# Moving the load of the next unit's fields from the end of a unit to behind its second layer, on three engines

## The chip, the cores and the metric

The kernel runs on one core of a Trainium2 chip. The metric is the device time of one execution in microseconds (us); lower is better. Five engines work side by side, each with an instruction stream of its own: TensorE (PE in the profile, its weight loads are PEld), VectorE (DVE), ScalarE (ACT), GpSimd (POOL) and SyncE (SP, here only DMAs). A "q" behind an engine's name (PEldq, ACTq) marks work of the engine's sequencer, which handles registers, branches and semaphore waits and hands instructions to the engine.

## The reference

The layer is a cross attention with sigmoid scores and a mixture of experts behind it, each gated and added to its input. Cut to the part in which the change lies:

```python
# M = 2048 tokens, H = 512, E = 16 experts, TOP_K = 4
t = norm(x) * norm_w
vals, idx = top_k(t @ gate_w.T + gate_b, 4)
gates = softmax(vals)                                  # scattered to G[M, E]
h = einsum('mh,eoh->emo', t, w1) + b1                  # first layer, 1024 outputs
a = minimum(h[..., ::2], 7); b = clip(h[..., 1::2], -7, 7)
act = a * sigmoid(1.702 * a) * (b + 1)                 # 512 hidden values
y = einsum('emi,edi->emd', act, w2) + b2               # second layer
out = x + tanh(g) * einsum('me,emd->md', G, y)
```

The kernel computes an expert only for the tokens that chose it.

## The kernel before, in words

The first 170 us hold the attention, the norms, the router, and the building of a table of token lists. Then comes the stage of the experts: a loop over units (`e.Fori(0, n)`, n is 24 here) that PE, ACT, DVE and POOL each run on their own. A unit is up to four tiles of 128 tokens of one expert. Because the lists are only known at run time, each engine reads a unit's fields (expert, slot of the second layer's weights, whether it is the expert's last unit, number of tiles, width, row) from a table `te` in SBUF into registers, with one load (`load_fields`, line 259). It keeps three sets of registers: `was` (the unit before), `now` and `nxt`. At the end of a unit `was` takes `now`, `now` takes `nxt`, and `nxt` is loaded with the fields of unit u + 2.

In a unit TensorE works in this order. The first layer has four parts, i = 0 to 3; a part is two groups (h = 0 and 1) of 12 matmuls (line 553; 32-bit numbers are split into a high and a low piece, so 4 x 3 products), whose width is 256 to 512 tokens. The code of a part exists once for each of six widths, and three compares and branches choose it (line 565). Inside part 0, and behind parts 0, 1 and 2, `turned_in(0..3)` turns a tile of tokens for the unit after this one (four transposes, line 479), if that unit has it. Behind part 0 stands `second_layer`, which is the second layer of the unit before: 12 matmuls of 512 columns for each of its tiles (line 500). All turned tiles go through one PSUM bank, `PX`: the transposes of tile j + 1 wait (line 477) until VectorE has read tile j out of it.

ScalarE in a unit: copy the biases (760), sigmoid part `sg` (720) and linear part `bw` (724) of part 0 with the copy of turned tile 0 (`high_x`, 683) between them; `second()`, that is the casts of the second layer's weights in a new expert (730) and then `gated` for each tile of the unit before (702, which waits for VectorE's bias add 1048); then `turned_in(1)` (683 again), the cast of a quarter of the next expert's first weights in an expert's last unit (`next_high`, 749), `kept(0)` (744), and the same for parts 1 to 3. VectorE follows it: bias add of the second layer's tiles (1048), low piece of a turned tile (`low_x`, 1023), the two steps of the activation (1075, 1077), low piece of the hidden values (`low_h`, 1081) and of the weights (1086). GpSimd gathers the tiles of tokens (1171) for `turned_in` and scatters the results (1228).

The order on each engine is that of the code; there is no scheduler. The lines that the change moves are 574 to 578 on TensorE, 778 to 782 on ScalarE and 1118 to 1122 on VectorE. GpSimd has its own set of registers and is not touched.

Of the kernel before, what the change touches and what calls it, by code (L numbers as in the profile page):

```python
# [19 lines left out]
E = 16  # L20
# [33 lines left out]
F_X, F_S2, F_LAST, F_NT, F_HL, F_ROW = range(6)  # L54
# [26 lines left out]
def build(nc, x, ctx, ctxT, gx, gf, nw, gw, gb, wts, bias, b1t, cst, out):  # L81
    with ExitStack() as es:
# [175 lines left out]
        def load_fields(e, regs, t, a):  # L258
            e.reg_load(regs, te[0:1, t:t + 1, a:a + len(regs)] if isinstance(t, int) else te[0:1, bass.ds(t, 1), a:a + len(regs)])
# [118 lines left out]
        def pe(e):  # L378
# [146 lines left out]
            with e.Fori(0, n) as u:  # L525
                par = e.snap(u % 2)
                x_ = e.snap(now[F_X], min_val=0, max_val=E - 1)
                wide = e.snap(now[F_HL], min_val=1, max_val=16)
                more = e.snap(nxt[F_NT], min_val=0, max_val=4)
                def turned_in(j):  # L530
                    with e.If(more > LESS[j]):
                        e.reg_add(turned, turned, 1)
                        e.reg_add(landed[j], landed[j], 16)
                        come, free = e.snap(landed[j], min_val=16, max_val=16 * NTILES), e.snap(turned, min_val=5, max_val=NTILES + 24)
                        e.wait_ge(d_g[j], come)
                        turn_x(j, free)

                ready = e.snap(e.snap(turned, min_val=4, max_val=NTILES + 24) + 1)
                for i in range(4):
                    made, read = e.snap(x_ * N1 + (i + 1)), e.snap(u * 4 + (i + 1))  # L540
                    e.wait_ge(e_lo1, made)
                    e.wait_ge(e_af, read)
                    e.wait_ge(e_bf, read)
                    e.sem_inc(e_gp, 1)

                    def part(w):
                        if i == 0:
                            e.wait_ge(e_xl, ready)
                        for h, P_, q in ((0, PA, e_l1a), (1, PB, e_l1b)):
                            t = 0  # L550
                            for k in range(4):
                                for xl, wl in PASSES:
                                    m = e.matmul(P_[i % 2][:, 0:32 * w], (W1h, W1l)[wl][:, i, 2 * k + h, :],  # L553
                                                 (xTh, xTl)[xl][:, bass.ds(par, 1), k, 0:32 * w], start=(t == 0), stop=(t == 11))
                                    t += 1
                            m.then_inc(q, 1)
                            if i == 0 and h == 0:
                                turned_in(0)

                    def pick(ws):  # L560
                        if len(ws) == 1:
                            part(ws[0])
                        else:
                            mid = len(ws) // 2
                            with e.If(wide <= ws[mid - 1]):
                                pick(ws[:mid])
                            with e.Else():
                                pick(ws[mid:])

                    pick(WIDTHS)  # L570
                    if i == 0:
                        second_layer(e.snap(u * 4 + 4))
                    if i < 3:
                        turned_in(i + 1)
                for a, q in zip(was, now):
                    e.reg_mov(a, q)
                for a, q in zip(now, nxt):
                    e.reg_mov(a, q)
                load_fields(e, nxt, e.snap(u + 2), 0)
            second_layer(e.snap(n * 4 + 4))  # L580


# [1 line left out]
        def act(e):  # L584
# [122 lines left out]
            with e.Fori(0, n) as u:  # L707
# [29 lines left out]
                def turned_in(i):  # L737
                    with e.If(more > LESS[i]):
                        e.reg_add(turned, turned, 1)
                        high_x(i, e.snap(turned, min_val=5, max_val=NTILES + 24), bass.ds(odd, 1))  # L740
# [21 lines left out]
                e.sem_inc(e_ga, 1)  # L762
                by_width(lambda w: gate(0, w, lambda: turned_in(0)))
                second()
                turned_in(1)
                next_high(0)

# [7 lines left out]
                        kept(i, w)  # L775

                by_width(pairs)
                for a, q in zip(was, now):
                    e.reg_mov(a, q)
                for a, q in zip(now, nxt):  # L780
                    e.reg_mov(a, q)
                load_fields(e, nxt, e.snap(u + 2), 0)
            e.wait_ge(e_dg, e.snap(n + 1))
            e.sem_inc(e_ga, 1)
            back = e.snap(was[F_NT], min_val=0, max_val=4)
# [6 lines left out]
        def dve(e):  # L792
# [257 lines left out]
            with e.Fori(0, n) as u:  # L1050
# [51 lines left out]
                turned_in(0)  # L1102
                by_width(lambda w: hidden(0, w))
                second()
                turned_in(1)

                def pairs(w):
# [7 lines left out]
                        low_w(i)  # L1115

                by_width(pairs)
                for a, q in zip(was, now):
                    e.reg_mov(a, q)
                for a, q in zip(now, nxt):  # L1120
                    e.reg_mov(a, q)
                load_fields(e, nxt, e.snap(u + 2), 0)
            side = e.snap(was[F_S2], min_val=0, max_val=1)
            back = e.snap(was[F_NT], min_val=0, max_val=4)
            come = e.snap(e.snap(was[F_X], min_val=0, max_val=E - 1) * 16 + 16)
# [171 lines left out]
```

## Time and profile before

| | |
|---|---|
| time, median of 3 runs | 821.39 us (820.71 to 821.41) |
| the profiled execution | 826.44 us, of which the span from the first to the last instruction is 824.5 us |
| PE busy | 766.4 us, 93% of the span |
| weight loads (PEld) | 653.8 us, 79% |
| DVE, ACT, POOL busy | 463.4, 417.9, 304.1 us |
| DMA | 117.02 MB, mean 142 GB/s |
| granted TensorE clock | mean 0.973; below full in one slice of the start and at the very end |

How to read it: PE is busy nearly throughout, with the other engines half busy beside it. The modelled end of a matmul lies behind the start of the next one, so a short stop of PE does not show as idle time of PE; it shows in the starts of the weight loads. In the unit loop one weight load begins for every matmul, so a stop is a distance between two starts beyond the usual one: 0.12 us at 256 columns, 0.13 at 288, 0.17 at 384, 0.20 at 448 and 0.23 at 512, read off between neighbouring weight loads. Units are counted from 0 in the texts; unit 0 begins at 173 us, unit 8 at 414, unit 11 at 497, unit 21 at 733, and unit 23, the last, at 779 us.

### The profile page before, as it was taken

The numbers are of one execution on the slowest core, as the hardware profiler recorded it, in microseconds if no ns is written. First come the engines' busy times: TensorE is split into PE (matmuls) and PEld (weight loads), VectorE is DVE, ScalarE is ACT, GpSimd is POOL, SyncE is SP. The second block draws the span as 40 slices with busy tenths as digits, with TensorE's granted clock in tenths as the row PEclk, the third lists the DMA queues.
The fourth block names the chain that finished last, engine by engine and source line by source line (L and its number), as shares of the span: only waits on it lengthen the run. The fifth ranks groups of instructions, "written<-read, shape, count | busy, mean of one in ns | idle before, by whom it ended". The sixth has DMA issues, their size and how long they took to land.

```text
span 824.5 us, 16539 instructions
## 1 busy us (share of the span) xinstructions
PE 766.4 (93%) x4067; PEld 653.8 (79%) x4068; DVE 463.4 (56%) x927; ACT 417.9 (51%) x691; POOL 304.1 (37%) x287
## 2 busy tenths in 40 slices
PE   8999996189999999999998999999999999999984
PEld 3666754178889889988887988898998888898873
DVE  3899885337556554556457555547346464646431
ACT  4577553036546454555556545537355554546431
POOL 0157766622332423421521443323342243325212
PEclk9999997599999999999999999999999999999997
DMA  8657743235757755655847864637545464544323
GB/s 288 222 191 231 237 122 113 43 105 154 168 128 225 155 124 140 127 149 156 205 92 212 216 131 102 156 99 175 127 90 144 99 181 115 159 115 76 38 26 39
DMA packets 107768, 117.02 MB, mean 142 GB/s; under 512 B 11808, under 2 KB 77344, under 8 KB 107744
## 3 DMA queue, kind: packets, MB, share of 16 engines
q1 hardware_dynamic: 88896, 77.32, 30.5%
q0 software_dynamic: 18848, 39.40, 24.7%
q8 instruction: 12, 0.20, 0.1%
q14 instruction: 12, 0.10, 0.0%
HBM read 88.06 MB, written 28.94 MB: 142 GB/s over the span
## 4 chain that ended last, share of the span: by engine, by line
PE 82%; issue 7%; DVE 3%; DMA 3%; ACT 2%; POOL 1%; ACTq 0%; DVEq 0%; POOLq 0%; another core or an unknown queue 0%; SPq 0%
PE ps L553 40%; PE ps L500 24%; PE ps L408 7%; PE ps L396 5%; PE ps L479 4%; DMA xg<-rows,srcI 2%; PE ps L425 1%; DVE W1l L1086 1%; PE ps L391 1%; PE ps L416 1%; POOL out L1228 1%; DVE bv L1075 0%; ACT bw L724 0%; DMA ys<-rows,src 0%; DVE ps L1048 0%
## 5 line engine op out<-in xcount | busy, mean ns | idle before, releaser
L553 PE MATMUL ps<-xTh,W1h 128*128 x768 | 257.8, 336 | 12.0 <-issue 6.5
L553 PE MATMUL ps<-xTh,W1l 128*128 x768 | 250.3, 326 | 0.0
L553 PE MATMUL ps<-xTl,W1h 128*128 x768 | 250.2, 326 | 0.0
L1228 POOL DMA_INDIRECT out<-ys,dgI x75 | 118.5, 1580 | 311.9 <-ACT ys L702 292.3
L553 PEld LDWEIGHTS ps<-xTh,W1h 128*128 128x128 f32 x768 | 144.6, 188 | 22.1 <-issue 17.6
L553 PEld LDWEIGHTS ps<-xTh,W1l 128*128 128x128 f32 x768 | 144.6, 188 | 5.1
L553 PEld LDWEIGHTS ps<-xTl,W1h 128*128 128x128 f32 x768 | 144.9, 189 | 4.5
L702 ACT ACTIVATE ys<-ps,dgI 128x512 f32<-128x512 f32 x75 | 51.8, 690 | 142.1 <-DVE ps L1048 138.1
L500 PE MATMUL ps<-W2h,hTh 128*128 x300 | 118.5, 395 | 3.4 <-DVE hTl L1081 3.2
L500 PE MATMUL ps<-W2h,hTl 128*128 x300 | 118.1, 394 | 0.0
L500 PE MATMUL ps<-W2l,hTh 128*128 x300 | 118.0, 393 | 0.0
L1023 DVE TENSOR_TENSOR xTl<-ps,xTh 128x512 f32 (+1 forms) x75 | 51.7, 691 | 93.4 <-ACT xTh L683 92.1
L1048 DVE TENSOR_TENSOR ps<-ps,b2s 128x512 f32<-128x512 f32 x75 | 52.4, 698 | 90.8 <-PE ps L500 89.9
L724 ACT ACTIVATE bw<-ps,bcur 128x384 f32<-128x384 f32 (+2 forms) x96 | 57.3, 596 | 86.0 <-PE ps L553 69.6
L1171 POOL DMA_INDIRECT xg<-rows,srcI x71 | 75.9, 1069 | 39.2 <-issue 37.9
L1075 DVE TENSOR_SCALAR bv<-bw 128x384 f32<-128x384 f32 (+2 forms) x96 | 35.9, 374 | 86.2 <-ACT bw L724 76.4
L1151 POOL DMA_INDIRECT tab<-C,dst x64 | 69.4, 1084 | 36.2 <-DVE dst L902 18.9
L1081 DVE TENSOR_TENSOR hTl<-hv,hTh 128x384 fp32r<-128x384 f32 (+2 forms) x96 | 55.2, 575 | 38.6 <-ACT hTh L744 33.9
L1086 DVE TENSOR_TENSOR W1l<-W1f,W1h 128x1024 fp32r<-128x1024 f32 x60 | 73.1, 1218 | 0.0
L720 ACT ACTIVATE sg<-ps,bcur 128x384 f32<-128x384 f32 (+2 forms) x96 | 57.3, 597 | 25.3 <-PE ps L553 12.8
L500 PEld LDWEIGHTS ps<-W2h,hTh 128*128 128x128 f32 x300 | 57.0, 190 | 15.6 <-issue 4.2
L500 PEld LDWEIGHTS ps<-W2l,hTh 128*128 128x128 f32 x300 | 57.0, 190 | 12.1
(147 smaller groups left out, 951.7 us busy)
## 6 DMA issues: line engine op xcount, KB each, us to landing
W1f<-in_wts SPq DMA_DIRECT2D x64, 512.0 KB
W2f<-in_wts SPq DMA_DIRECT2D x32, 512.0 KB
X<-in_x SPq DMA_DIRECT2D x8, 512.0 KB, 6.5
Kt<-in_ctx SPq DMA_DIRECT2D x8, 512.0 KB
Vt<-in_ctxT SPq DMA_DIRECT2D x8, 512.0 KB
rows<-tt SPq DMA_DIRECT2D x8, 512.0 KB
out<-base SPq DMA_DIRECT2D x8, 512.0 KB
b2s<-in_bias SPq DMA_DIRECT2D x16, 256.0 KB
```

Source lines behind the costliest of these rows:

```text
L408: m = e.matmul(ps[2 + j][:], Vt[b % 2][:, c, 128 * j:128 * j + 128], Sc[:, c, :], start=(c == 0), stop=(c == 3))
L500: m = e.matmul(PY[j][:], (hTh, hTl)[hl][:, c, 128 * j:128 * j + 128], (W2h, W2l)[wl][:, bass.ds(slot, 1), H * c:H * c + H], start=(t == 0) ...
L553: m = e.matmul(P_[i % 2][:, 0:32 * w], (W1h, W1l)[wl][:, i, 2 * k + h, :], (xTh, xTl)[xl][:, bass.ds(par, 1), k, 0:32 * w], start=(t == 0) ...
L702: e.activation(ys[j][:], PY[j][:], AF.Copy, scale=dgI[:, j, 1:2]).then_inc(e_ys, 1)
L720: e.activation(sg[i % 2][:, 0:w], PA[i % 2][:, 0:w], AF.Silu, scale=ALPHA, bias=bcur[:, 2, i:i + 1]).then_inc(e_af, 1)
L724: e.activation(bw[i % 2][:, 0:w], PB[i % 2][:, 0:w], AF.Identity, scale=1.0 / ALPHA, bias=bcur[:, 1, i:i + 1]).then_inc(e_bf, 1)
L1048: e.tensor_tensor(PY[j][:], PY[j][:], b2s[:, bass.ds(side, 1), :].rearrange("p o h -> p (o h)"), ALU.add).then_inc(e_yb, 1)
L1081: e.tensor_tensor(hTl[:, i, 0:w], hv[i % 2][:, 0:w], hTh[:, i, 0:w].bitcast(F32), ALU.subtract).then_inc(e_hl, 1)
L1086: e.tensor_tensor(W1l[:, i, :, :], W1f[:, i, :, :], W1h[:, i, :, :].bitcast(F32), ALU.subtract).then_inc(e_lo1, 1)
L1151: e.indirect_dma_start(tab, bass.IndirectOffsetOnAxis(dst[:, b, q:q + 1], axis=0), pay[:, 2 * b + q // K, q % K, :], None).then_inc(d_put, 16)
L1171: e.indirect_dma_start(xg[j][:], None, rows, bass.IndirectOffsetOnAxis(srcI[:, j, 0:1].bitcast(I32), axis=0)).then_inc(d_g[j], 16)
L1228: e.indirect_dma_start(out, bass.IndirectOffsetOnAxis(dgI[:, j, 0:1].bitcast(I32), axis=0), ys[j][:], None, compute_op=ALU.add).then_inc(d ...
```

## The change

Register moves and the load of `nxt` leave the end of the loop's body and stand behind the second layer (TensorE, in part 0) and behind `second()` (ScalarE, VectorE). What is read from `now` and `nxt` after that point is read from `was` and `now`.

```diff
@@ pe
                     if i == 0:
                         second_layer(e.snap(u * 4 + 4))
+                        for a, q in zip(was, now):
+                            e.reg_mov(a, q)
+                        for a, q in zip(now, nxt):
+                            e.reg_mov(a, q)
+                        load_fields(e, nxt, e.snap(u + 2), 0)
+                        x_ = e.snap(was[F_X], min_val=0, max_val=E - 1)
+                        wide = e.snap(was[F_HL], min_val=1, max_val=16)
+                        more = e.snap(now[F_NT], min_val=0, max_val=4)
                     if i < 3:
                         turned_in(i + 1)
-                for a, q in zip(was, now):
-                    e.reg_mov(a, q)
-                for a, q in zip(now, nxt):
-                    e.reg_mov(a, q)
-                load_fields(e, nxt, e.snap(u + 2), 0)
@@ act, and the same in dve
                 second()
+                for a, q in zip(was, now):
+                    e.reg_mov(a, q)
+                for a, q in zip(now, nxt):
+                    e.reg_mov(a, q)
+                load_fields(e, nxt, e.snap(u + 2), 0)
+                x_ = e.snap(was[F_X], min_val=0, max_val=E - 1)
+                nt = e.snap(was[F_NT], min_val=1, max_val=4)
+                more = e.snap(now[F_NT], min_val=0, max_val=4)
+                last = e.snap(was[F_LAST], min_val=0, max_val=1)
                 turned_in(1)
...
                 by_width(pairs)
-                for a, q in zip(was, now):
-                    e.reg_mov(a, q)
-                for a, q in zip(now, nxt):
-                    e.reg_mov(a, q)
-                load_fields(e, nxt, e.snap(u + 2), 0)
```

TensorE, around the second layer: the last matmul of its fourth tile, the branch out of it, and the first turned tile behind it (`C` and `xg` are the identity and the gathered tokens).

```order
 L500 MATMUL ps<-W2l,hTh 128x512
 L488 UNCONDITIONAL_BRANCH
+L574 ISA x2
+L576 ISA
+L259 TENSOR_LOAD te
+L578 ISA
 L531 COMPARE_AND_BRANCH
 L532 ISA
 L479 MATMUL ps<-C,xg_66 128x128 x4
```

The load now stands between the second layer and the transposes of `turned_in(1)`, with four register instructions around it.

TensorE, at the end of the loop's body, behind the last matmul of part 3:

```order
 L553 MATMUL ps<-xTh,W1l 128x512
 L567 UNCONDITIONAL_BRANCH
-L576 ISA
-L578 ISA x2
-L259 TENSOR_LOAD te
 L525 REGISTER_ALU
 L525 COMPARE_AND_BRANCH
```

What is left there is the loop's own counting and branch.

ScalarE, behind `gated` of the fourth tile (`ys`), before the change:

```order
L702 ACTIVATE ys_64<-ps,dgI 128x512
L734 UNCONDITIONAL_BRANCH
L738 COMPARE_AND_BRANCH
L739 ISA
L683 ISA
L683 COPY xTh<-ps 128x4x128
```

and after it (lines of the changed file; 702, 734, 738, 739 and 683 have become 705, 737, 741, 742 and 686):

```order
L705 ACTIVATE ys_64<-ps,dgI 128x512
L737 UNCONDITIONAL_BRANCH
L769 ISA
L259 ISA
L259 TENSOR_LOAD te
L773 ISA
L741 COMPARE_AND_BRANCH
L742 ISA
L686 ISA
L686 COPY xTh<-ps 128x4x128
```

The load stands between the last `gated` and the copy of turned tile 1 out of `PX`; on VectorE it stands in the same way between the last bias add and `low_x(1)`.

## Rows read from the trace of the kernel before

**Rows 1.** The page, part 4: shares of the chain that ended last
```profile
PE 82%; issue 7%; DVE 3%; DMA 3%; ACT 2%; POOL 1%; ACTq 0%; DVEq 0%; POOLq 0%; another core or an unknown queue 0%; SPq 0%
```

**Rows 2.** Waits of the weight loads: who <- whom: us in total, times, longest us
```profile
PEld ps L553 <- issue: 17.6, 23, 1.4
```

**Rows 3.** Sequencer work of lines 259 and 779: ns min/median/max, starts
```profile
L259 PEldq TENSOR_LOAD <-te x26: 586/929/1242, 156.1 to 796.2; - x26
L259 DVEq TENSOR_LOAD <-te x26: 347/666/1018, 156.4 to 801.1; - x26
L259 ACTq TENSOR_LOAD <-te x26: 315/614/917, 166.5 to 800.4; - x26
...
L779 ACTq FUSED_REGOPS  x24: 171/171/171, 197.8 to 800.1; - x24
```

**Rows 4.** Line 259 in narrow windows: PE in units 10 and 11, ACT in 11
```profile
L259 PEldq TENSOR_LOAD <-te x1: 588/588/588, 494.5 to 494.5; - x1
...
L259 PEldq TENSOR_LOAD <-te x1: 1242/1242/1242, 515.2 to 515.2; - x1
...
L259 ACTq TENSOR_LOAD <-te x1: 899/899/899, 519.1 to 519.1; - x1
```

**Rows 5.** Timeline of weight loads at unit ends: start, us, what [idle before]
```profile
495.79 0.19 PEld L553 LDWEIGHTS ps<-xTh,W1l 128*128 128x128 f32 x1
496.82 0.19 PEld L553 LDWEIGHTS ps<-xTh,W1h 128*128 128x128 f32 x1 [0.85 <-issue]
...
441.16 0.19 PEld L553 LDWEIGHTS ps<-xTh,W1h 128*128 128x128 f32 x1 [0.83 <-issue]
...
518.00 0.19 PEld L553 LDWEIGHTS ps<-xTh,W1h 128*128 128x128 f32 x1 [1.20 <-issue]
```

**Rows 6.** The same, start of part 2 in unit 11
```profile
509.46 0.49 PEld L479 LDWEIGHTS ps<-C,xg 128*128 128x128 f32 x4
510.45 0.19 PEld L553 LDWEIGHTS ps<-xTh,W1h 128*128 128x128 f32 x1 [0.50 <-issue]
```

**Rows 7.** Line 734 in a narrow window, then timeline of ACT and DVE, unit 11
```profile
L734 ACTq COMPARE_BRANCH  x2: 50/50/50, 507.0 to 507.2; - x2
...
507.04 0.69 ACT L702 ACTIVATE ys<-ps,dgI 128x512 f32<-128x512 f32 x1 [1.97 <-DVE ps L1048]
507.71 0.59 ACT L683 CAST xTh<-ps 128x512 f32 x1
...
508.60 0.69 DVE L1023 TENSOR_TENSOR xTl<-ps,xTh 128x512 f32 x1 [1.60 <-ACT xTh L683]
```

**Rows 8.** Timeline: gather and turned tile 0 of units 9 and 11; unit 17
```profile
439.05 1.03 POOL L1171 DMA_INDIRECT xg<-rows,srcI  x1 [1.03 <-issue]
...
445.20 0.42 PEld L479 LDWEIGHTS ps<-C,xg 128*128 128x128 f32 x4 [1.71 <-DMA xg<-rows,srcI]
...
491.48 1.03 POOL L1171 DMA_INDIRECT xg<-rows,srcI  x1 [1.02 <-issue]
...
498.38 0.49 PEld L479 LDWEIGHTS ps<-C,xg 128*128 128x128 f32 x4
...
644.67 0.42 PEld L479 LDWEIGHTS ps<-C,xg 128*128 128x128 f32 x4 [0.34 <-DMA xg<-rows,srcI]
```

**Rows 9.** Timeline of unit 21 on ACT and DVE, and the second layer behind it
```profile
746.20 0.69 ACT L702 ACTIVATE ys<-ps,dgI 128x512 f32<-128x512 f32 x1 [2.03 <-DVE ps L1048]
...
754.48 0.51 ACT L744 CAST hTh<-hv 128x384 fp32r<-128x384 f32 x1 [0.73 <-DVE hv L1077]
...
755.37 0.57 ACT L724 ACTIVATE bw<-ps,bcur 128x384 f32<-128x384 f32 x1
...
758.16 0.56 DVE L1081 TENSOR_TENSOR hTl<-hv,hTh 128x384 fp32r<-128x384 f32 x1 [0.58 <-ACT hTh L744]
...
759.33 0.19 PEld L500 LDWEIGHTS ps<-W2h,hTh 128*128 128x128 f32 x1
```

**Rows 10.** Timeline of weight loads: part 1 of unit 0, which has no second layer
```profile
180.03 0.19 PEld L553 LDWEIGHTS ps<-xTh,W1h 128*128 128x128 f32 x1 [1.31 <-issue]
```

More of the change, by code:

```diff
@@ L1104, in dve @@
                 second()
+                for a, q in zip(was, now):
+                    e.reg_mov(a, q)
+                for a, q in zip(now, nxt):
+                    e.reg_mov(a, q)
+                load_fields(e, nxt, e.snap(u + 2), 0)
+                x_ = e.snap(was[F_X], min_val=0, max_val=E - 1)
+                nt = e.snap(was[F_NT], min_val=1, max_val=4)
+                more = e.snap(now[F_NT], min_val=0, max_val=4)
+                last = e.snap(was[F_LAST], min_val=0, max_val=1)
                 turned_in(1)
@@ L1117, in dve @@
                 by_width(pairs)
[L1118 to L1122, printed above, removed]
             side = e.snap(was[F_S2], min_val=0, max_val=1)
```

## The prediction, made before the changed kernel ran

> **What bounds the kernel now.** I read the chain that ended last first: 82% of it is PE, and 7% is "issue", time in which nothing that the profile knows was waited for [rows 1]. PE is the bound, and what an engine beside it does counts only where PE stops. So the second view is that of the waits of the weight loads: line 553 stopped 23 times for "issue", 17.6 us in all [rows 2]. The third is the timeline of the weight loads over the unit loop, to see where these stops lie. They lie in three places: at the ends of units [rows 5], at the start of part 2 behind turned tile 2 [rows 6], and once in unit 0 [rows 10]. The fourth is the sequencer's own load, line 259: on PE it takes 0.59 or 1.24 us, on ACT 0.32 or 0.9 [rows 3]. The two values alternate: units 0, 2, 4 ... have the short one and units 1, 3, 5 ... the long one, as unit 10 and unit 11 show [rows 4].
>
> The stop at the end of a unit is the sequencer running late. In unit 10 its load starts at 494.5 [rows 4], 1.3 us before the last weight load of the unit at 495.79; with the branch and the moves ahead of it the sequencer is some 1.75 us, 15 matmuls of 0.12 us, ahead. Then come the load, the loop branch, three compares and the first address, and the first weight load of unit 11 stands 1.03 us behind the last instead of 0.12 [rows 5]. In wide units the same 15 matmuls last 2.6 to 3.5 us, and there is little or no stop.
>
> **What goes at the unit ends.** The block that leaves PE's chain there is the load and about 0.41 us of moves and gaps between them: 1.0 us in even units, 1.65 in odd ones. The loss at a unit end is the idle time, plus 0.19 (a weight load), less the usual distance. Over the 23 unit ends: 0.24 and 0.05 (units 1, 3), 0.89 (5), 0.89 (8), 0.92 (10), 1.25 (11), 1.25 (13), 0.41 (15), 0.92 (16), 1.10 (17), 0.92 (18), 1.25 (19), 1.10 (21), 1.06 (22); nothing at the other nine (those of units 10, 8 and 11 are in [rows 5]). The sum is 12.3 us. Each is smaller than the block that goes, so on PE alone all of it goes. What is late next:
> - Units 8 and 16 are followed by a wait of turned tile 0 for its gather, 1.71 and 0.34 us [rows 8]. If PE arrives earlier it waits longer. Their 0.89 and 0.92 give nothing.
> - The second layer of the next unit needs the low hidden values of part 3. Behind unit 21 it starts 0.6 us after they are done (758.72 against 759.33 [rows 9]; the least such distance in the trace is 0.24), so of 1.10 at most about 0.4 could be had. Behind unit 17 it starts as soon as it can: nothing of the 1.10.
>
> The other ten give 8.2 us.
>
> **What the new place costs on PE.** Behind the second layer the sequencer is further ahead, since its matmuls take 0.23 us each and four transposes follow. In the tightest units with two tiles to do (11, 17, 19) I count from the last branch of the second layer (502.4 us in unit 11) 1.75 for the block, 0.3 to the transposes and some 1.2 to the first address of part 1: about 505.8 against 506.3, when part 1 starts. So 0.5 us of slack at the least, and I take zero. The bound above is the long block without cover, 1.65 us a unit. Unit 0 has no second layer, and its part 1 starts late already [rows 10]; most of its block hides behind the wait for `PX`, and I take 0.2.
>
> **What it costs through ScalarE and VectorE.** This is the term that decides. Part 2 of a narrow unit cannot start until turned tile 2 is in PE's queue; that waits for `PX`, and this for VectorE's line 1023, which waits for ScalarE's 683, which stands right behind the last `gated` (702). In unit 11: 702 starts at 507.04, 683 at 507.71, 1023 at 508.60 and ends at 509.29, the transposes begin at 509.46, and part 2 at 510.45 after 0.50 of idle time [rows 6, 7]. From the end of 1023 to part 2 it is 1.15 us, with nothing in it that the change touches. The changed ScalarE does 0.17 of moves, the load and some 0.2 of small ones between 702 and 683: about 0.73 us in even and 1.3 in odd units [rows 3, 4]. All of it starts when 702 starts, and some of it lies beside 702, which takes 0.69: in unit 11 the copy can start 0.67 after 702 now. With the branches of tiles that a unit lacks, the delay is 0.46 (four tiles) and 0.6 (three) in even units and 1.2 in odd ones. VectorE's load is done before ScalarE's copy and adds nothing.
>
> Units whose part 2 stops there today pay all of it: 8 and 10 (0.46 each), 16, 18 and 22 (0.61 each), 11, 13 and 19 (1.25, 1.21, 1.25), 6.5 us together. The units with 384 columns have 0.6 us of room: unit 5 pays 0.6, units 4, 12, 14 and 20 nothing. Wider units have over 1 us. Back comes what falls in front of a gather that is late anyway: 0.46 of unit 8 and 0.61 of unit 16. Unit 21 has no turned tile 2, but its ScalarE and VectorE work without a break, 3.14 us a part against 3.17 of PE (744 waits 0.73 for 1077, then 720, 724, 749 follow without idle time [rows 9]); a delay of 1.2 at part 1 is still there at its end. Its second layer then starts 0.7 later than today. Unit 17 has the same chain, but there 724 of part 3 started late for no reason that I can name, so I take zero for it.
>
> Sum: ends -8.2, unit 21 +0.7, part 2 +6.5, unit 5 +0.6, unit 0 +0.2, back -1.1: -1.3 us on the profiled 826.44. The median of the runs is 5 us lower; I carry the difference over as it is: 821.39 - 1.3 = 820.1.
>
> The Trainium skill states something that speaks against the 6.5 us (Advanced Engine Details and Errata, Sequencer and Instruction Queues): an engine's instructions are pushed into a queue, 8 deep at ScalarE and VectorE, and wait for their semaphores there, while the sequencer reads on. By that rule ScalarE's sequencer would pass 702 while it waits for VectorE and have the load done before 702 starts, and the delay would be none. The timeline doesn't show it so: the sequencer's first branch behind 702 begins at 507.0, with 702 itself, after ScalarE had been idle 1.97 us [rows 7]. For TensorE the same section gives 64; the trace has about 15 matmuls with their weight loads, some 31.
>
> **The rivals.**
> - A: the ScalarE delay is hidden. For it speaks that ACT is idle 1.97 us before 702 [rows 7], time enough for the whole block if the sequencer passes the waiting 702; against it the branch at 507.0. Then nothing of the 6.5, 0.6 and 0.7 is paid: 8.2 + 0.4 - 0.2 - 0 = 8.4 us, 813.0. This is what the rule above would give. If half is hidden, some 817.
> - B, slower: the load on ScalarE waits until 702 is finished, 0.65 us more in every unit. The copy of tile 1 then comes 1.1 to 1.9 us later, each of the eight narrow units pays 0.65 more (5.2), the five of 384 columns 0.5 (2.5): 820.1 + 7.7 = 827.8. It decides from a mean delay of about 1 us in the narrow units on, against the 0.8 that I count. Against it: at the end of unit 11 the load on ACT starts at 519.1 [rows 4] while line 744 is running.
> - C: the gains at the ends are taken by the gathers in more units. A gather takes 6.1 us from its issue at 439.05 until PE is let go at 445.20; in unit 11 (and 19 is alike) the tile's turn comes 6.9 us after the issue, at 498.38 [rows 8]. That leaves 0.8 us of room, less than the 0.92 that PE gains in front of it; later landings there would take up to 1.8 us, and PE's slack of 0.5 us in the units with two tiles may not be there, up to 0.3 in three of them: 820.1 + 1.8 = 821.9, to 823.
> - That the stops at the unit ends stay because the branches cause them is excluded by their size: with the block gone, what is left of the sequencer's way is 1.5 us against 1.8 to 2.0 of lead.
>
> **How the numbers follow.** A measurement of this kernel can tell about 0.2%, 1.6 us, from no change. The forecast has 0.53, with its own range 818.3 to 821.9; A 0.18; C 0.16; B 0.13. The range 816.0 to 824.0 takes in the forecast, C, the half-hidden form of A and the mild form of B. Faster by over 0.2% (under 819.75): all of A and 0.20 of the forecast, 0.38. Within 0.2%: 0.30 of the forecast and 0.12 of C, 0.42. Slower: B, 0.04 of C and 0.03 of the forecast, 0.20.
>
> **What the profile after would show.** The weight loads' stops at unit ends [rows 5] are gone, except in front of late gathers, whose waits have grown by up to 0.9 us [rows 8]. The stops in front of part 2 [rows 6] have grown, from 0.4 or 0.5 to about 0.9 in units 8, 10, 16, 18, 22 and to 1.7 in units 11, 13, 19; unit 5 has a new one. Between 702 and 683 lie 1.1 to 1.4 us in even units and 1.7 to 1.9 in odd ones instead of 0.6 to 0.67 [rows 7]. No stop in front of part 1 outside unit 0. If part 2's stops haven't grown, A holds; if they have grown to over 1.3 in even units, B. A stop in front of part 1 would make the PE part wrong.

## The result: slower by 0.7%, outside the range

| | before | after |
|---|---|---|
| time, median of 6 runs each | 821.40 us (819.67 to 821.77) | 826.36 us (825.09 to 830.71) |
| ratio | | 1.0067, 95% interval 1.0050 to 1.0084 |
| the profiled execution, and its span | 826.44, 824.5 us | 825.09, 823.3 us |
| PE busy | 766.4 us | 764.5 us |
| mean granted clock | 0.973 | 0.977 |

820.1 us was forecast, with a range of 816 to 824. The changed kernel takes 5.0 us more than the one before.

### Two profiles that must not be subtracted as they are

The two profiled executions differ by 825.09 - 826.44 = -1.35 us, which is almost the forecast's -1.3, and means nothing. I measured three stretches of the program in every profile: up to the first weight load of unit 0, from there to the first weight load of part 3 of unit 23, and from the start of the first to the end of the last of the 36 weight loads of the last second layer:

| us | ahead of the unit loop | the loop to unit 23, part 3 | last second layer, 36 weight loads |
|---|---|---|---|
| before | 172.96 | 621.55 | 10.88 |
| before, profiled again | 171.37 | 622.56 | 9.64 |
| after | 169.82 | 626.26 | 8.02 |

Only the middle column can feel the change much. The first varies between 169.5 and 173.4 us over all thirteen profiles, the last takes 8.0, about 9.6 or 10.9 us whatever the kernel. Beside the profile of the changed kernel, the one before had fallen badly in both, by 3.1 and 2.9 us. The last column is the clock. Of the kernel before, the busy time by stretch (sum of each engine in the window, then PE's granted clock, DMA share, GB/s):

```profile
800.00:806.00 6.00, 4.67 (x11) 3.72 (x12) 0.56 (x1) 0.49 (x1) 0.00 (x0) 0.55 0.00 0
806.00:812.00 6.00, 6.00 (x24) 4.84 (x24) 1.40 (x2) 1.38 (x2) 1.56 (x1) 0.88 0.16 14
```

and of the changed one:

```profile
800.00:806.00 6.00, 3.07 (x14) 2.56 (x15) 1.48 (x3) 1.03 (x2) 0.00 (x0) 1.00 0.00 0
806.00:812.00 6.00, 5.37 (x24) 4.13 (x22) 1.88 (x3) 1.38 (x2) 2.52 (x2) 1.00 0.28 34
```

Behind part 3 of the last unit PE stands idle for 3.4 us, waiting for the last hidden values. In the first of the two executions it then ran its first 15 of 36 matmuls at the lower level of 1.2 GHz (0.55 is the mean of that window), a weight load every 0.43 us; in the second all of them at 2.4 GHz, one every 0.23 us. So all comparisons below are of the loop, and of the medians of the timed runs. The loop says +4.7 us and the medians +5.0.

### What the profile of the changed kernel shows

Shares of the chain that ended last, by engine, and then by line:

```profile
PE 82%; DVE 5%; issue 4%; POOL 2%; ACTq 2%; ACT 2%; DMA 2%; DVEq 0%; POOLq 0%
PE ps L553 39%; PE ps L500 25%; PE ps L408 7%; PE ps L396 5%; PE ps L479 3%; POOL tab L1162 2%; ACTq L259 1%; PE ps L425 1%; DVE ps L1055 1%; PE ps L391 1%; DVE xTl L1030 1%; PE ps L416 1%; ACT xTh L686 1%; ACT hTh L747 1%; DVE hv L1084 1%
```

Against [rows 1], "issue" has gone from 7 to 4%, and DVE from 3 to 5 and ACTq from 0 to 2% have come in its place. Three lines are new among those listed: ScalarE's load (L259), its copy of a turned tile (L686, 683 before) and VectorE's low piece of it (L1030, 1023 before).

The waits (who <- whom: us in total, times, longest us):

```profile
PEld ps L479 <- issue: 10.3, 10, 2.0
PEld ps L553 <- issue: 10.1, 16, 1.4
PEld ps L500 <- issue: 7.8, 5, 3.3
```

Line 553 stops for 10.1 us in place of 17.6 [rows 2]. The transposes (479), which are queued behind the wait for `PX`, have 10.3.

The end of unit 10, in the timeline of weight loads (start, us, what, idle before), and the start of part 2 of unit 11:

```profile
493.73 0.19 PEld L553 LDWEIGHTS ps<-xTh,W1l 128*128 128x128 f32 x1
493.85 0.19 PEld L553 LDWEIGHTS ps<-xTh,W1h 128*128 128x128 f32 x1
...
508.57 0.42 PEld L479 LDWEIGHTS ps<-C,xg 128*128 128x128 f32 x4 [2.00 <-issue]
509.62 0.19 PEld L553 LDWEIGHTS ps<-xTh,W1h 128*128 128x128 f32 x1 [0.63 <-issue]
```

At the end of the unit the next weight load comes after 0.12 us, where it was 1.03 [rows 5]: the stop is gone. In the middle the transposes now wait 2.00 us. From the start of unit 11 to the last line it is 15.77 us, against 510.45 - 496.82 = 13.63 before [rows 5, 6]: 2.14 lost to gain 0.91.

ACT and DVE in that place of unit 11:

```profile
504.09 0.69 ACT L705 ACTIVATE ys<-ps,dgI 128x512 f32<-128x512 f32 x1 [1.96 <-DVE ps L1055]
506.88 0.58 ACT L686 CAST xTh<-ps 128x512 f32 x1 [2.09 <-issue]
```
```profile
507.76 0.69 DVE L1030 TENSOR_TENSOR xTl<-ps,xTh 128x512 f32 x1 [3.70 <-ACT xTh L686]
```

The copy starts 2.79 us behind the start of 705, where it was 0.67 [rows 7]. Between them is the load. Its lengths (ns min/median/max, first and last start), over the program, and then the one of unit 11:

```profile
L259 ACTq TENSOR_LOAD <-te x26: 314/616/1906, 163.2 to 790.9; - x26
...
L259 ACTq TENSOR_LOAD <-te x1: 1624/1624/1624, 504.8 to 504.8; - x1
```

It lasts 1.62 us. The same load at the end of the unit lasted 0.90 [rows 4]; the longest of before was 0.917 [rows 3]. In even units it is 0.32 as ever: unit 10 after the change has

```profile
484.48 0.69 ACT L705 ACTIVATE ys<-ps,dgI 128x512 f32<-128x512 f32 x1 [2.03 <-DVE ps L1055]
485.63 0.59 ACT L686 CAST xTh<-ps 128x512 f32 x1 [0.46 <-issue]
```

that is 1.15 us from start to start. In odd units the load now lasts 1.24 us (1, 3 and 7, whose second layer has four tiles), 1.6 (two or three tiles) or 1.9 (unit 9), in place of 0.9 in all of them.

### The profile page after: what moved, and what is told of

Its sections match the earlier page's. It is cut to its first block, busy times and chain, and to the rows that moved or that the text cites. A ratio compares the mean times of both kernels' runs of the same rounds, so it can differ in the third digit from the quotient of the medians.

```text
span 823.3 us, 16635 instructions
## 1 busy us (share of the span) xinstructions
PE 764.5 (93%) x4067; PEld 652.1 (79%) x4068; DVE 462.8 (56%) x927; ACT 417.9 (51%) x691; POOL 304.7 (37%) x287
## 4 chain that ended last, share of the span: by engine, by line
PE 82%; DVE 5%; issue 4%; POOL 2%; ACTq 2%; ACT 2%; DMA 2%; DVEq 0%; POOLq 0%
PE ps L553 39%; PE ps L500 25%; PE ps L408 7%; PE ps L396 5%; PE ps L479 3%; POOL tab L1162 2%; ACTq L259 1%; PE ps L425 1%; DVE ps L1055 1%; PE ps L391 1%; DVE xTl L1030 1%; PE ps L416 1%; ACT xTh L686 1%; ACT hTh L747 1%; DVE hv L1084 1%
## 5 line engine op out<-in xcount | busy, mean ns | idle before, releaser
L553 PEld LDWEIGHTS ps<-xTh,W1h 128*128 128x128 f32 x768 | 144.8, 188 | 14.8 <-issue 10.1
L1030 DVE TENSOR_TENSOR xTl<-ps,xTh 128x512 f32 (+1 forms) x75 | 51.7, 691 | 103.4 <-ACT xTh L686 101.2
L686 ACT CAST xTh<-ps 128x512 f32 (+1 forms) x75 | 43.8, 585 | 54.3 <-issue 27.6
```

The costliest lines, as they stand in the source:

```text
L1030: e.tensor_tensor(xTl[:, par, :, 128 * j:128 * j + 128], P_[:].rearrange("p (c t) -> p c t", c=4), xTh[:, par, :, 128 * j:128 * j + 128].b ...
```

## The experiments

"Loop" is the change of the middle column above against the kernel before, in one profiled execution. Medians are of five to seven runs of each kernel, beside 11 or 13 runs of the kernel before on the same chip (821.31 us for the four behind the changed kernel, 820.89 for the next four, 822.47 for the last ones).

| kernel | time | ratio, 95% interval | loop |
|---|---|---|---|
| changed | 826.36 | 1.0067 (1.0050 to 1.0084) | +4.7 |
| TensorE's block moved alone | 814.62 | 0.9910 (0.9892 to 0.9928) | -5.2 |
| ScalarE's and VectorE's moved alone | 837.62 | 1.0197 (1.0182 to 1.0212) | +16.7 |
| all but VectorE's | 827.82 | 1.0077 (1.0059 to 1.0095) | +6.7 |
| all but ScalarE's | 814.20 | 0.9921 (0.9900 to 0.9942) | -7.7 |
| TensorE's alone, 32-byte rows | 811.62 | 0.9883 (0.9865 to 0.9902) | -10.3 |
| changed, 32-byte rows | 817.68 | 0.9956 (0.9937 to 0.9975) | -3.7 |
| changed, ScalarE's block one step later | 817.04 | 0.9950 (0.9932 to 0.9968) | -5.8 |
| before, 32-byte rows | 816.53 | 0.9947 (0.9930 to 0.9963) | -5.1 |
| changed, ScalarE loads early | 817.73 | 0.9927 (0.9901 to 0.9953) | -7.1 |
| the same, 32-byte rows | 817.09 | 0.9937 (0.9913 to 0.9962) | -8.1 |

### Which engine's move costs

The first four take the change apart by engine. TensorE's block moved alone (the diff is the change's own, in `pe`; `act` and `dve` are as before):

```diff
@@ pe
                         second_layer(e.snap(u * 4 + 4))
+                        ... (the moves and the load)
                     if i < 3:
                         turned_in(i + 1)
-                ... (the moves and the load)
```

> The move on TensorE alone; ScalarE and VectorE load their fields at the end of the unit, as in the kernel before. Theory D (the loss comes through ScalarE: its load delays the copy of turned tile 1 out of PX, and with it part 2): all stops at unit ends stay gone (-12.2 us against before), part 2 starts as before (0), the second layers of units 18 and 22 start as before, two gathers and two late hidden values take back some 3 us: about 812.5 us, ratio 0.989. Theory P (the block behind the second layer costs TensorE itself what it saves at the unit end): no gain, 821 us or more, with stops in front of part 1 or part 2.

Measured: 814.62 us. The stops at the unit ends are all gone (-12.2 us in the loop), nothing comes in front of part 2 (0.1 in all). What is given back stands between the start of part 0 and the end of the second layer, +5.8 us. 4.0 of it are gathers that are late now (unit 9 +1.2, unit 11 +0.9, unit 17 +0.7, unit 18 +0.8, unit 19 +0.3). Late hidden values give +0.7 in unit 22 and -0.4 in unit 18, where the gather's wait lies in front of theirs. Another 0.6 is in front of part 1 of unit 0.

The last 1.6 us, all in unit 9, are TensorE's clock. PE has waited 2.90 us for the gather when it starts again, and soon after that the granted clock is at its lower level of 1.2 GHz for a while:

```profile
441.96 0.42 PEld L479 LDWEIGHTS ps<-C,xg 128*128 128x128 f32 x4 [2.90 <-DMA xg<-rows,srcI]
```
```profile
442.00:444.00 2.00, 2.00 (x11) 1.85 (x12) 0.40 (x1) 0.59 (x1) 0.00 (x0) 0.82 0.96 290
444.00:446.00 2.00, 2.00 (x7) 1.78 (x6) 0.30 (x1) 0.00 (x0) 0.00 (x0) 0.50 0.10 29
```

There the weight loads are 0.37 us apart in place of 0.20. In the kernel before, the wait at this place was 1.71 us [rows 8] and the clock stayed at 2.4 GHz.

ScalarE's and VectorE's blocks alone:

```diff
@@ act, dve
                 second()
+                ... (the moves and the load)
                 turned_in(1)
@@ end of the body of act, dve
-                ... (the moves and the load)
```

> The move on ScalarE and VectorE alone; TensorE as before. Theory D: the stops at unit ends stay (0), part 2 comes 11 to 12 us later in all as in the changed kernel, and units 18 and 22 start their second layer some 2 us late each, less 1 us that falls before a late gather: about 835 us, ratio 1.016. Theory P: about as before, 821 us, for then the two engines are not what costs.

Measured: 837.62 us. In front of part 2 it loses 11.9 us, as much as the whole change does (11.7), and nothing changes at the unit ends (+0.2). The price in front of part 2 and the gain at the unit ends are thus two separate things: the price is ScalarE's or VectorE's, the gain TensorE's.

The totals don't add up so simply: -5.2 and +16.7 us in the loop would make +11.5, and the whole change has +4.7. In this profile, too, PE falls to 1.2 GHz inside the loop, twice, about the start of part 2 of units 11 and 13. Both stretches of 3.4 us have a granted clock of 0.50:

```profile
511.70:515.10 3.40, 2.96 (x13) 2.95 (x13) 3.37 (x7) 2.49 (x5) 2.08 (x2) 0.50 0.60 132
566.30:569.70 3.40, 3.40 (x16) 3.40 (x15) 3.33 (x6) 1.97 (x3) 2.07 (x3) 0.50 0.62 165
```

Inside these two parts the weight loads are 0.24 us apart in place of 0.13, which costs 2.9 us. No other profile than these two has such a stretch in the loop. So 4.5 of the 6.8 us are the clock of the two profiled executions. Gathers that are late only where TensorE's gain comes without ScalarE's delay make another 3.6, and late hidden values, which wait longer in the whole change, take 1.9 of it back. The medians don't add up either (-6.7 and +16.3 against +5.0), but they can't tell how often the clock fell in the other executions.

Everything moved but VectorE's block, which stays at the end:

```diff
@@ dve
                 second()
-                ... (the moves and the load)
                 turned_in(1)
@@ end of the body
+                ... (the moves and the load)
```

> The changed kernel with VectorE's load back at the end of the unit (ScalarE's and TensorE's behind the second layer). In odd units ScalarE's load took 1.24 to 1.9 us in the changed kernel and 0.9 before. Theory O (the two loads overlap, and ScalarE's waits for VectorE's): ScalarE's load is back at 0.9 in odd units, part 2 of units 11, 13, 19 comes 0.7 earlier each than in the changed kernel, and the chains of units 17 and 21 too: 4 to 5 us less than the changed kernel, about 822 us. Theory B2 (the load is long because a bias-scaled copy, 705, runs beside it): it stays at 1.6, and the time at 826.

Measured: 827.82 us, which can't be told from the changed kernel. Its loop is 2.0 us longer in the profile, but 1.3 of that is a gather (in front of the second layer of unit 9) and 0.3 is unit 0; in front of part 2 the two agree to 0.2 us. So VectorE's move is worth little or nothing, and ScalarE's load is as long as with it:

```profile
L259 DVEq TENSOR_LOAD <-te x26: 349/666/979, 152.4 to 804.6; - x26
L259 ACTq TENSOR_LOAD <-te x26: 312/660/1903, 163.2 to 792.9; - x26
```

No load of any other engine lies beside ScalarE's long ones here (the nearest starts 3.7 us or more away), so the theory that two loads in one place collide falls. TensorE's isn't the partner either: with its load at the unit end, in the experiment above, ScalarE's odd loads are 1.23 to 1.91 us too.

Everything moved but ScalarE's block:

```diff
@@ act
                 second()
-                ... (the moves and the load)
                 turned_in(1)
@@ end of the body
+                ... (the moves and the load)
```

> The changed kernel with ScalarE's load back at the end of the unit (VectorE's and TensorE's behind the second layer). Theory D: VectorE's load is hidden behind ScalarE's 705 and 686 (they take 2 us from the last bias add, the block 1.1 to 1.35), so the time is that of the move on TensorE alone, about 812.5 us. If VectorE's load delays its line 1030 as well: up to 5 us more, 817.

Measured: 814.20 us, the same as with TensorE alone. In front of part 2 it is +0.4 us. All of the loss there is ScalarE's.

### The length of the load

The table `te` has 24 bytes a row. A row is read with one load; rows 32 bytes apart change nothing else:

```diff
-        te = sb("te", [128, NUP, 6], I32)
+        te = sb("te", [128, NUP, 8], I32)
...
-            e.tensor_tensor(te[:].rearrange("p t r -> p r t"), ...
+            e.tensor_tensor(te[:, :, 0:6].rearrange("p t r -> p r t"), ...
```

With TensorE's block alone moved:

> The move on TensorE alone, and the rows of the table te 32 bytes apart instead of 24. Theory M (a load from a row at an odd place, 24 bytes further, is long because of where it starts): all loads of line 259 are short, 0.32 on ScalarE, 0.35 on VectorE, 0.59 on TensorE. The loads of ScalarE and VectorE at the end of a unit are hidden, and TensorE's behind the second layer too, so the time is that of the move on TensorE alone, 814.6 us, within 2. Theory N (the long ones have another cause): the loads stay at 0.9 and 1.24 in every second unit; same time.

Measured: 811.62 us, the fastest of all. The alternation is gone, and ScalarE and VectorE have short loads only:

```profile
L259 PEldq TENSOR_LOAD <-te x26: 578/583/1014, 151.3 to 771.1; - x26
L259 DVEq TENSOR_LOAD <-te x26: 341/354/369, 151.5 to 787.6; - x26
L259 ACTq TENSOR_LOAD <-te x26: 306/311/328, 163.1 to 786.9; - x26
```

against 586 to 1242, 347 to 1018 and 315 to 917 [rows 3]. TensorE's longest, 1014 ns, belongs to unit 2, an even one: behind the second layer its loads of units 1 to 4 and 7 take 0.66 to 1.01 us, and the rest 0.58 to 0.61. Beside the same kernel with 24-byte rows the loop gains 5.0 us: 2.9 in unit 9, of which 1.3 are the gather's wait and 1.6 the clock that stays at 2.4 GHz, 0.9 each in front of late gathers in units 11 and 17, 0.3 in unit 19, and 0.5 in unit 0. Of this 0.3 is lost again in small steps of unit 9.

The whole change with these rows:

> The changed kernel with the rows of te 32 bytes apart. Theory M: ScalarE's load is 0.32 in every unit, the copy of turned tile 1 is late by 0.65 instead of some 2 us in odd units; part 2 of units 11, 13, 19 comes 1.3 to 1.4 earlier each than in the changed kernel, units 1, 3 and 5 lose their stop (1.9 together), the chains of units 17 and 21 with the second layers behind them give 3 to 4 back; some of it is taken by late gathers: about 818 us. Theory N: no change, 826.

Measured: 817.68 us. In front of part 2 it is 5.8 us less than in the changed kernel: 1.27, 1.34 and 1.25 in units 11, 13 and 19, 1.28 in unit 5, 0.3 and 0.4 in units 1 and 3, nothing in the even ones. ScalarE's loads are these:

```profile
L259 ACTq TENSOR_LOAD <-te x26: 308/314/328, 163.1 to 782.2; - x26
```

1.3 us is 1.62 - 0.31, the excess of the long load. Its length thus goes one to one into the path.

The kernel before with these rows:

> The kernel before with the rows of te 32 bytes apart, nothing moved. Theory M: TensorE's load at the end of odd units takes 0.59 instead of 1.24, so the stops there shrink by up to 0.65: 0.24 and 0.05 in units 1 and 3, 0.65 each in 5, 11, 13 and 19, 0.4 in 15, and in 17 and 21 what the late hidden values leave, 0 and 0.5; even units as before: 3.8 us less, 817.5 us. Theory N: 821 us.

Measured: 816.53 us. The unit ends give 4.7 us, 0.6 to 0.7 behind each odd unit that had a stop of more than that, and the whole stop where it was smaller (units 1, 3 and 15: 0.25, 0.04 and 0.41). That is the difference of TensorE's 1.24 and 0.59. It is a sizeable gain without any move.

### The way into part 2

ScalarE's block stands one step later, behind `turned_in(1)`, so that nothing is between 705 and the copy out of `PX`:

```diff
@@ act
                 second()
-                ... (the moves and the load)
                 turned_in(1)
+                ... (the moves and the load)
                 next_high(0)
```

> The changed kernel with ScalarE's block behind turned_in(1) instead of ahead of it; VectorE and TensorE as changed. Theory X (the delay of part 2 comes through PX, that is through the copy 686 which stands behind the block): part 2 starts as in the kernel before (11.7 us less than changed), while the late chains of units 17 and 21 remain (second layers of 18 and 22 some 2 us late each): about 818 us. Theory Y (any 1 to 2 us of ScalarE's time in this half of the unit costs the same): 826 us.

Measured: 817.04 us. The loads are no shorter:

```profile
L259 ACTq TENSOR_LOAD <-te x26: 312/726/1782, 163.4 to 780.6; - x26
```

Yet of the 11.7 us in front of part 2 11.3 are gone (unit 11 -1.96, 13 -2.03, 19 -1.97). So the loss goes through the copy of turned tile 1 and `PX`, and not through ScalarE's later work. The late second layers of units 18 and 22 stay as they are in the changed kernel (0.0 of difference): these come through ScalarE's chain of activations, in which the block stands either way.

ScalarE loads into a spare set of registers ahead of the second layer's activations, and only moves registers behind them:

```diff
@@ act
+            spare = many_regs(e, "act_spare", 4)
...
+                load_fields(e, spare, e.snap(u + 2), 0)
                 second()
                 ... (was takes now, now takes nxt)
-                load_fields(e, nxt, e.snap(u + 2), 0)
+                for a, q in zip(nxt, spare):
+                    e.reg_mov(a, q)
```

> The changed kernel, but ScalarE loads into a spare set of registers ahead of the second layer's activations, where it waits for VectorE anyway (1.97 us in unit 11 before), and behind them only moves registers: 12 moves instead of 8 moves and the load. Theory X (the extra time is the load's own length behind the last activation of the second layer): the copy of tile 1 comes only some 0.3 us later than in the kernel before, so the 11.7 us in front of part 2 fall to 2 or 3, the late chains of units 17 and 21 to under 1, and the time is about 815 to 817. Rival Z (ScalarE's sequencer does not get past the load until it has finished something else, or the load delays the activations themselves): the activations start later instead, and the time stays at 822 to 826. On the length: if the odd loads last 1.24 to 1.9 us because the second layer's activations (512 columns out of PSUM) run beside them, they last 0.9 us here; if it is the stretch inside a unit that lengthens them, they last 1.2 to 1.6 here too.

Measured: 817.73 us, 0.7 above the 815 to 817 of theory X, and far from Z's. (The kernel before took 822.47 beside it, 1.1 more than beside the changed kernel.) In front of part 2 2.6 us are left of 11.7: 0.2 in units 8 and 10, 0.3 to 0.45 in the others. In unit 11 the load and the activations behind it stand as follows:

```profile
L259 ACTq TENSOR_LOAD <-te x1: 897/897/897, 499.1 to 499.1; - x1
```
```profile
499.22 0.60 ACT L728 ACTIVATE bw<-ps,bcur 128x384 f32<-128x384 f32 x1
502.58 0.69 ACT L706 ACTIVATE ys<-ps,dgI 128x512 f32<-128x512 f32 x1 [2.77 <-DVE ps L1058]
505.23 0.69 ACT L706 ACTIVATE ys<-ps,dgI 128x512 f32<-128x512 f32 x1 [1.96 <-DVE ps L1058]
...
506.30 0.59 ACT L686 CAST xTh<-ps 128x512 f32 x1 [0.37 <-issue]
```

The load lasts 0.90 us, in the middle of the unit, with activations of 384 columns beside it, and so do all the odd ones (0.90 to 0.92). It is ready 2.5 us before the first activation is let go. So being inside a unit doesn't lengthen it. What does belongs to what stands behind the second layer's activations; behind `turned_in(1)` it was 1.62 to 1.78 us.

The same with 32-byte rows:

> The same with the rows of the table 32 bytes apart. Every load is then short (ScalarE 0.31, VectorE 0.35, TensorE 0.59 us). Expected: nothing is lost in front of part 2 beyond 0.2 us a unit, the gathers of units 9, 11 and 17 come as in the TensorE-only kernel with 32-byte rows (811.6), so about 811 to 813. If it is clearly below 811, ScalarE's and VectorE's own move has a value that the TensorE-only kernel lacks; if above 814, moving ScalarE's registers inside the unit costs by itself.

Measured: 817.09 us, outside the 811 to 813 that I expected. Its loop is 2.1 us longer than that of TensorE's block alone with 32-byte rows. In front of part 2 it is 2.4 longer, 0.3 to 0.4 in each of six narrow units and 0.2 in the other two: register moves in front of the copy cost on ScalarE even when no load is among them. The early load was right, its address made no difference any more (817.73 and 817.09 can't be told apart), and the moves keep the price.

### The kernel before, once more

> The kernel before once more, for its profile alone. The stretch ahead of the loop took 173.0 us in the first profiled execution and 169.5 to 170.8 in every profile since. If that was chance, it takes about 170 us here, the span is about 820.5 to 821.5, and the unit loop is the same to within 1 us (weight-load starts at the unit ends and in front of part 2 within 0.05 us each). If the 173 us belong to the kernel before, it takes 173 us again, and the change would have gained 3 us ahead of the loop.

Measured: 824.64 us in one run, with 171.4 us ahead of the loop and 9.6 in the last second layer; the loop is 1.0 us longer than in the first profile, all of it in front of the second layers of units 9, 11 and 19 (+0.25, +0.45, +0.33), which follow gathers. The unit ends and part 2 are the same to within 0.1 us each. So two of the three things that I compare are steady, and a gather's wait is known to half a microsecond only.

## Why the prediction was wrong

By its own terms, in the loop:

| term | predicted | measured |
|---|---|---|
| ten unit ends | -8.2 | -8.2 |
| part 2 of the narrow units and unit 5 (and 1 and 3, +0.7, not foreseen) | +7.1 | +11.7 |
| ends of units 8 and 16, with the gathers behind | -1.1 | -3.3 |
| unit 17 and the second layer behind it | 0 | +1.4 |
| unit 21 and the second layer behind it | +0.7 | +1.6 |
| unit 0 | +0.2 | +0.9 |
| not foreseen, the rest | 0 | +0.6 |
| sum | -1.3 | +4.7 |

- **The unit ends: right.** All fourteen stops are gone, 12.2 us of the 12.3 that I had summed; the ten that were to be kept gave 8.2.
- **TensorE's new place: right outside unit 0.** No part 1 but that of unit 0 starts later, by more than 0.05 us. That holds although TensorE's own load grew to 2.0 us in units 1, 3 and 7. Unit 0 lost 0.3 in front of part 1 and 0.6 in front of part 3.
- **VectorE's block: right.** It costs nothing that shows (all of the change but VectorE's block is no faster).
- **The way through ScalarE, 683 and `PX` into part 2: right as a mechanism, mis-sized.** This is the step that failed: "the changed ScalarE does 0.17 of moves, the load and some 0.2 of small ones between 702 and 683: about 0.73 us in even and 1.3 in odd units". The even units paid 0.54 to 0.76 where 0.46 to 0.61 stood, 3.4 in all against 2.75: the branches and moves are 0.08 to 0.15 longer than I had summed. The odd ones paid 2.0 to 2.1 where 1.2 stood, and units 1, 3 and 5 together 2.0 where 0.6 stood: 8.2 against 4.3. I had carried the load's 0.9 us from the end of the unit to the place behind 702, and it isn't 0.9 there. With 1.62 in its place the odd units come to 1.9 or 2.0, and with the 0.15 of the even ones to 2.1, which is what they paid. The prediction had taken the duration from where the load stood and set no upper bound on it, and its row for PE, 1242 in one engine against 917 in another, was the only sign that the length depends on more than the address.
- **Late chains: too small.** Unit 17 has in fact the chain of unit 21, and both lose more: the odd load is 0.7 longer here too, and the copy in `turned_in(1)` comes before everything else that ScalarE does in the unit. The second layers behind them start 1.6 and 2.0 us later. Behind unit 21:

```profile
760.42 0.56 DVE L1088 TENSOR_TENSOR hTl<-hv,hTh 128x384 fp32r<-128x384 f32 x1 [0.58 <-ACT hTh L747]
```
```profile
761.21 0.19 PEld L500 LDWEIGHTS ps<-W2h,hTh 128*128 128x128 f32 x1 [1.96 <-issue]
```

The weight load waits 1.96 us, and comes 0.79 behind the start of the low hidden values. Before, these came 1.17 apart [rows 9].
- **Gathers: too dark.** Units 8 and 16 kept 2 us that I had given away; the second layer behind unit 8 even started 1.1 earlier after its unit's start. PE is late by part 2's delay when it gets there, and the gather isn't. With TensorE's block alone, where there is no such delay, the gathers take 4.0 us: 1.9 in units 9 and 17, where the forecast had given 1.8 away, and 2.0 in units 11, 18 and 19, about the 1.8 of rival C. The forecast had no term for the clock: the longest of these waits is followed by 3.4 us at the lower level, which cost another 1.6 us.

Of the rivals, A is excluded: the delay was not hidden, though ACT is idle 1.96 us ahead of 705. The Trainium skill (Advanced Engine Details and Errata, Sequencer and Instruction Queues) lets the sequencer read on past a waiting instruction; the experiment with the early load shows that ScalarE's does get ahead of its waiting activation with what stands in front of it (load at 499.1, activation at 502.6), while in the changed kernel the first thing that the sequencer does behind the last activation, a branch or a register move, begins 0.01 us after that activation in all 23 units, never before it. By the rule the block would have cost nothing, and here the measurement decides. The sequencer does read ahead where an instruction has nothing left to wait for and only the engine is busy. In unit 11 of the changed kernel a branch (741) of `turned_in(2)` is taken up at 507.55, although three activations and copies stand in front of it in the code and start only later, without idle time between them:

```profile
L741 ACTq COMPARE_BRANCH  x1: 34/34/34, 507.6 to 507.6; - x1
```
```profile
508.30 0.51 ACT L747 CAST hTh<-hv 128x384 fp32r<-128x384 f32 x1
508.72 0.58 ACT L723 ACTIVATE sg<-ps,bcur 128x384 f32<-128x384 f32 x1
509.19 0.58 ACT L727 ACTIVATE bw<-ps,bcur 128x384 f32<-128x384 f32 x1
```

So in these rows it is the wait for another engine that holds the sequencer, and not the instruction in front of it as such.

B had nearly the right time, 827.8, and the wrong reason. It had the load wait for the end of 702, 0.65 us more in every unit. But the load doesn't wait for that end: it begins 0.33 us behind the start of the last 705 where the second layer has four tiles, 0.50 where three and 0.68 where two, which is the price of the branches over missing tiles (unit 10: 484.8 against 484.48). The excess is in the odd units alone, and goes with the length of the load. C is real, but is outweighed.

The range of 816 to 824 missed the result by 2.4 us since it took the load's length from one place as fixed. With 0.7 us more in each of the eight odd units that pay (1, 3, 5, 11, 13, 17, 19, 21) it would have reached some 829.

What stays open: why a long load lasts 1.24 to 1.9 us behind the second layer and 0.9 at the unit's end and ahead of the second layer. Neither VectorE's nor TensorE's load is the partner, as shown, and it isn't a thing of the middle of a unit as such. The lengths 0.32, 0.91, 1.24, 1.6 and 1.9 stand in steps of about 0.3 us, and the load is shorter (1.24) where the second layer has four tiles than where it has two or three (1.6, once 1.9), that is where ScalarE has just branched over code. That is a correlation; no run took the branches away. Nor are the engines independent: with only ScalarE's load moved ahead of the second layer, TensorE's loads of units 1, 3 and 7 took 1.34 to 1.50 us in place of 1.96 to 2.02 in the changed kernel. What they share is not shown.

## What to carry to other kernels

A register load belongs where its own engine waits for nobody and nobody waits for it, and each engine has a place of its own: here TensorE's behind the second layer (-0.9%), ScalarE's at the unit's end, where it was hidden. One edit on three engines joined a gain of 6.7 us (TensorE's block alone) to a loss of some 12 (826.36 against 814.20 without ScalarE's). A wait that grows can also cost more than its own length, as the 1.6 us at the lower clock behind the gather of unit 9 show. A time taken from one place isn't a bound for another, so a moved instruction that stands in front of a release should be priced with a range. And the table that a loop reads its registers from wants aligned rows: 32 bytes in place of 24 gave 0.5% to the kernel before and 1.1% to the changed one (0.9956 against 1.0067). No run tried another spacing, so 32 is what worked and not the least that would.

## What the runs showed of the hardware

- A load of registers from a table in SBUF has two lengths that follow the address: 0.32 and 0.91 us on ScalarE, 0.35 and 0.97 on VectorE, 0.59 and 1.24 on TensorE, for rows of 24 bytes in turn. With rows 32 bytes apart the alternation is gone on all three (0.31, 0.35 and 0.58 us in the kernel before with such rows).
- Such a load has no fixed length. Behind the second layer the long form grew to 1.9 us on ScalarE and 2.0 on TensorE. TensorE's short form grew there too, to 0.9 in units 2 and 4 of the changed kernel and to 1.0 with 32-byte rows; ScalarE's stayed at 0.32 in the changed kernel and had up to 0.54 behind `turned_in(1)`.
- ScalarE's sequencer does not get past an activation that waits for another engine (0.01 us behind its start in 23 of 23 units), but does get past several that are only queued (741 at 507.55 ahead of 747 at 508.30).
- TensorE's granted clock fell to 1.2 GHz for 3.4 us inside the loop in two profiles, once behind a wait of 2.90 us and twice at the start of part 2, behind transposes that had waited 2.01 and 1.79 us. At that level the weight loads of matmuls of 448 columns came 0.37 us apart in place of 0.20, and of 288 columns 0.24 in place of 0.13. Waits of 2.00 and 1.98 us in the changed kernel, and one of 2.41 us in that without ScalarE's block, were not followed by a fall.
- Two executions of one program, the kernel before, differ by 1.6 us ahead of the loop and by 1.2 in the last second layer; over all thirteen profiles, whose kernels differ little there, it is up to 3.9 and 2.9. In the last second layer PE comes out of 3.4 us of idle time and gets one clock or the other. A profile of one execution has to be cut into stretches before it is compared.
